# One unit of a state-space scan: the softplus on GpSimd placed behind its multiplications, the C row spread in bf16 parts, the projections paired

## The reference, cut to what matters

```python
xz = x @ in_w.T; xi, z = split(xz)
u = silu(conv(xi) + conv_b)                      # 4 taps along time, 512 channels
dt, Bm, Cm = split(u @ xproj_w.T)                # 16 + 16 + 16 numbers per token
delta = softplus(dt @ dt_w.T + dt_b)
dA = exp(delta * A); dBu = delta * Bm * u        # per channel and per state n = 0..15
h[t] = dA[t] * h[t-1] + dBu[t]; y[t] = sum_n h[t, n] * Cm[t, n]
out = (y + u * Dp) * silu(z) @ out_w.T
```

## Time and profile before

| | |
|---|---|
| time, median of 3 runs | 8230.42 us (8223.12 to 8230.87) |
| the profiled execution | 8213.02 us, its span 8211.7 us |
| busy share of the span | PE 81%, DVE 74%, POOL 48%, ACT 38% |
| granted TensorE clock, mean | 0.89 of full speed |

### The profile page before, as it was taken

The page is one execution under the profiler, slowest core; times in us unless marked ns, Lnnn a source line. Parts: engine busy times, 40 slices in busy tenths (PEclk is TensorE's granted clock), DMA queues, the critical chain, the costliest instruction groups (busy, mean ns, idle before and its releaser), DMA issues. The chain is left out here.

```text
span 8211.7 us, 61601 instructions
## 1 busy us (share of the span) xinstructions
PE 6631.6 (81%) x19212; PEld 3520.3 (43%) x19212; DVE 6111.6 (74%) x7134; ACT 3152.1 (38%) x6327; POOL 3927.4 (48%) x2745
## 2 busy tenths in 40 slices
PE   5888878887788877888778888788887888878887
PEld 3533354333543335433354333543345443444433
DVE  6488965888658885588855888658886588765887
ACT  0255512554125541255412554134531355313553
POOL 3166541665425654255542655426543365433564
PEclk8889898898888988989989999898998988988998
DMA  2000010001100011000110001100001000110001
GB/s 77 19 29 28 27 47 13 29 31 39 32 19 24 31 39 40 13 24 29 39 40 13 29 24 39 40 13 31 24 36 40 16 29 26 36 37 16 29 29 36
DMA packets 211678, 248.50 MB, mean 30 GB/s; under 512 B 140858, under 2 KB 168546, under 8 KB 205412
## 3 DMA queue, kind: packets, MB, share of 16 engines
q1 hardware_dynamic: 211300, 244.04, 9.0%
HBM read 223.98 MB, written 20.03 MB: 30 GB/s over the span
## 5 line engine op out<-in xcount | busy, mean ns | idle before, releaser
L1142 DVE TENSOR_TENSOR_SCAN wk<-ps,wk 128x1024 f32<-128x1024 f32 x1024 | 2333.6, 2280 | 267.9 <-POOL wk L1697 139.6
L1364 PE MATMUL ps<-wk,ident 128*128 128x512 f32 x4096 | 2368.2, 707 | 101.0 <-DVE wk L1163 101.0
L1692 POOL TENSOR_TENSOR wk<-wk 128x1024 f32<-128x1024 f32 x1024 | 2403.2, 2357 | 8.6
L1606 ACT ACTIVATE ps<-wk,Aneg 128x255 f32<-128x255 f32 x4096 | 1700.8, 462 | 1569.2 <-DVE wk L1142 1520.0
L1354 PE MATMUL ps<-wk,ident 48*128 48x256 f32 x2048 | 767.2, 457 | 909.2 <-DVE wk L1151 857.8
L1151 DVE TENSOR_TENSOR wk<-wk,ps 128x1024 f32<-128x1024 f32 x1024 | 1224.9, 1196 | 92.2 <-issue 37.4
L1364 PEld LDWEIGHTS ps<-wk,ident 128*128 128x128 f32 x4096 | 781.2, 211 | 1066.0 <-issue 1063.7
L403 POOL TENSOR_SCALAR rstd<-mv 128x4 f32<-128x4 f32 x146 | 36.1, 247 | 2342.8 <-DVE mv L396 2342.8
L1354 PEld LDWEIGHTS ps<-wk,ident 48*128 48x128 f32 x2048 | 320.6, 196 | 1394.0 <-DVE wk L1151 1243.6
L509 POOL TENSOR_TENSOR wk<-wk 128x4096 f32<-128x4096 f32 x64 | 529.4, 8278 | 294.6 <-ACT wk L631 294.6
L1645 POOL TENSOR_TENSOR wk<-wk 128x1024 f32<-128x1024 f32 x64 | 150.4, 2350 | 1067.1 <-ACT wk L1531 1067.1
(11 more groups left out here) (175 smaller groups left out, 7495.8 us busy)
## 6 DMA issues: line engine op xcount, KB each, us to landing
wk<-bc_scr SPq DMA_DIRECT2D x256, 512.0 KB, 3.6
wk<-in_wgT SPq DMA_DIRECT2D x8, 1536.0 KB, 6.6
wk<-in_wuT SPq DMA_DIRECT2D x8, 1536.0 KB, 9.6
wk<-in_wdn SPq DMA_DIRECT2D x8, 1536.0 KB, 6.5
wk<-in_x SPq DMA_DIRECT2D x18, 512.0 KB, 4.0
o_scr<-wk SPq DMA_DIRECT2D x64, 128.0 KB, 3.0
wk<-o_scr SPq DMA_DIRECT2D x32, 256.0 KB, 3.5
wk<-wf_scr SPq DMA_DIRECT2D x8, 1024.0 KB, 4.8
```

Of the source, the lines that this page charges most:

```text
L1142: V.tensor_tensor_scan(h, in_time(d, flat(decay(m))), h, 0.0, ALU.mult, ALU.add).then_inc(scanned, 1)
L1364: mm = nc.tensor.matmul(bank(j), ident[:], hc[m % RC][:, 2 * j:2 * j + 2, :].rearrange("p e t -> p (e t)"), start=(n == 0), stop=(n == DS ...
L1606: nc.scalar.activation(decay(m)[:, e, rest(d)], dl[g % 2][:, e, rest(d)], ACT.Exp, scale=Aneg[:, d, e, n:n + 1]).then_inc(dA_done, 1)
L1692: nc.gpsimd.tensor_tensor(hb[n], du[g % 2], col(Bb[j % 2][:, n % NB, :]) .broadcast_to([P, NDI, MC]), ALU.mult).then_inc(dbu, 1)
```

## The change

1. GpSimd: `POOL_PRE` is gone. The softplus of the next unit stands behind all 16 multiplications of the unit. The ScalarE and VectorE steps of the softplus move to steps 8 to 11 and to step 10 (`SUM`), behind `conv` of that step. The exponential of the carried factors (ACT, 64 elements) moves from step 0 of its unit to step 13 of the one before.
2. The C row: GpSimd splits rows 32 to 47 of `xd`, which `xpT` now repeats at rows 64 and 96, into three bf16 parts (`part_c`, five small instructions per unit), and `weights` multiplies them by a bf16 selection matrix `sel3` in one bf16 matmul where an f32 one stood.
3. The pieces: the four `LG` are two of 512 columns (steps 2, 3); the two `OUT` become one of 512 columns, made in four halves at steps 4 to 7 and read by one `out_evac` at step 9. `XD` is copied by ScalarE at its step 4, not 3; `LG` by four activations at steps 6 and 7.
4. The woven layer norm moves to steps 10, 12, 14 of unit 6 and 1, 4 of unit 7.
5. Once per launch: `xpT` is cleared by GpSimd and loaded by six DMAs where one was, behind the others.

```diff
-            PRE_PE = {0: (XD, 0), 3: (LG, 0), 4: (LG, 1), 5: (LG, 2), 6: (LG, 3), 8: (X, 0), ...
+            PRE_PE = {0: (XD, 0), 2: (LG, 0), 3: (LG, 1), 8: (X, 0), 9: (X, 1), 10: (X, 2),
-            Z_ACT, XD_ACT, LG_ACT = {0: 0, 1: 1, 2: 2, 3: 3}, 3, {7: 0, 8: 1, 9: 2, 10: 3}
-            OUT_PE, OUT_DVE = {1: 0, 2: 1}, {3: 0, 4: 1}
+            Z_ACT, XD_ACT, LG_ACT = {0: 0, 1: 1, 2: 2, 3: 3}, 4, {6: 0, 7: 1}
+            OUT_PE, OUT_DVE = {4: (0, 0), 5: (0, 1), 6: (1, 0), 7: (1, 1)}, 9
-            SOFT = {10: "abs", 11: "exp", 12: "ln", 13: "less"}
-            SILU, SUM = 15, 13
-            POOL_PRE = {13: ("lost",), 14: ("delta", "du")}
-            CLOSE_DVE = {5: ("stats0",), 7: ("apply0", "stats1"), 9: ("apply1",), 11: ("stats2",), 14: ("apply2",)}
-            CLOSE_POOL = {7: "rstd0", 10: "rstd1", 12: "add", 13: "rstd2"}
+            SOFT = {8: "abs", 9: "exp", 10: "ln", 11: "less"}
+            SILU, SUM, INJ = 15, 10, 13
+            CLOSE_DVE = {10: ("stats0",), 12: ("apply0", "stats1"), 14: ("apply1",), DS + 1: ("stats2",),
+                         DS + 4: ("apply2",)}
+            CLOSE_POOL = {DS + 1: "add", DS + 5: "rstd2"}
...
-                    def out_evac(g, t):
+                    def out_evac(g):
+                        dve.wait_ge(out_mm, g + 1)
+                        y = ytok[:, c * MT:(c + 1) * MT, :]
...
                     def weights(m):
                         if n == 0:
-                            pe.wait_ge(pre_ev, evacuated((XD, g, 0)))
+                            pe.wait_ge(c_part, NPART * (g + 1))
                         if m:
                             pe.wait_ge(cm, m)
-                        nc.tensor.matmul(c_row(), ident[0:XP, row:row + 1].broadcast_to([XP, P]), xd[g % 2][0:XP, :],
+                        nc.tensor.matmul(c_row(), sel3[:, n:n + 1].broadcast_to([XR, P]), xc[g % 2][0:XR, :],
                                          start=True, stop=True).then_inc(c_bc, 1)
...
+                    def part_c(g):
+                        x, parts = xd[g % 2], xc[g % 2]
+                        pool.wait_ge(pre_ev, evacuated((XD, g, 0)))
+                        if g >= 2:
+                            pool.wait_ge(c_bc, DS * (g - 1))
+                        nth = NPART * g
+                        nc.gpsimd.tensor_copy(parts[0:XR, :], x[0:XR, :]).then_inc(c_part, 1)
+                        for q in range(1, PARTS):
+                            rows = slice(XC[q], XR)
+                            pool.wait_ge(c_part, nth + 2 * q - 1)
+                            nc.gpsimd.tensor_tensor(xr[rows, :], (x if q == 1 else xr)[rows, :], parts[rows, :],
+                                                    ALU.subtract).then_inc(c_part, 1)
+                            pool.wait_ge(c_part, nth + 2 * q)
+                            nc.gpsimd.tensor_copy(parts[rows, :], xr[rows, :]).then_inc(c_part, 1)
+                        pool.wait_ge(c_part, nth + NPART)
...
-                            if g + 1 < NU:
-                                for what in POOL_PRE.get(n, ()):
-                                    softplus(g + 1, what)
+                        if g == CLOSE_UNIT:
+                            close_step(1, "rstd0", 0, 0)
+                        if g + 1 < NU:
+                            part_c(g + 1)
+                            for what in ("lost", "delta", "du"):
+                                softplus(g + 1, what)
+                        if g == CLOSE_UNIT:
+                            close_step(1, "rstd1", 0, 0)
```

More of the change, by code:

```diff
@@ L38 @@
 XP = DTR + 2 * DS
+XC = (DTR + DS, 64, 96)
+XR = XC[-1] + DS
 HF, RANK = 1024, 16
@@ L166, in build @@
         inj = [area(at + NDI * MC * RC + i * DS * NDI, DS, NDI) for i in range(2)]
+        at += NDI * MC * RC + 2 * DS * NDI
+        xc = [area(at + i * MC // 2, MC, dt=BF16) for i in range(2)]
+        xr = area(at + MC, MC)
         tt, tl = [area((120 + 4 * i) * KB, NDI, MC) for i in range(2)]
@@ L240, in _ @@
                     sp.dma_start(dst[:], src.broadcast_to([P, src.shape[1]])).then_inc(loaded, 16)
+                sp.wait_ge(blank, 1)
+                for dst, src in SPREAD:
+                    for d in range(2):
+                        sp.dma_start(dst[:, d], src[:, d]).then_inc(loaded, 16)
                 sp.wait_ge(loaded, NLOAD)
@@ L903, in pre_slot @@
                     at = 5 if AT[piece] < NFIRST and AT[piece] % 2 == 0 else 6
-                    return bank(at)[:, 0:XW if piece[0] == X else MC]
+                    return bank(at)[:, 0:{X: XW, LG: 2 * MC, OUT: MT * C}.get(piece[0], MC)]
                 def slot_before(piece):
@@ L1219, in _ @@
                                 finish(g - 1)
-                            if g and n in OUT_DVE:
-                                out_evac(g - 1, OUT_DVE[n])
+                            if g and n == OUT_DVE:
+                                out_evac(g - 1)
                             if g + 2 < NU and n in CONV:
@@ L1235, in _ @@
                         square(s)
-                    for t in range(MT):
-                        out_evac(NU - 1, t)
+                    out_evac(NU - 1)
                     squares = iter(range(UP_FIRST, NF))
-                    dve.wait_ge(out_ev, MT * NU)
+                    dve.wait_ge(out_ev, NU)
                     for name in ("stats0", "apply0", "stats1", "apply1", "stats2", "apply2"):
@@ L1330, in project @@
                             t0 = c * MC + t * P
-                            for k in range(KC):
-                                mm = nc.tensor.matmul(o, xnT[:, k, t0:t0 + P], PxT[:, k, :], start=False,
-                                                      stop=(k == KC - 1))
-                        mm.then_inc(out_mm, 1)
+                            mm = nc.tensor.matmul(o, xnT[:, half, t0:t0 + P], PxT[:, half, :], start=False,
+                                                  stop=(half == 1))
+                        if (t, half) == (MT - 1, 1):
+                            mm.then_inc(out_mm, 1)
                     def ahead_t(piece):
@@ L1462, in _ @@
                             piece = pe_piece(g, n)
-                            if piece:
+                            if g and n in OUT_PE:
+                                project(g - 1, *OUT_PE[n])
+                            elif piece:
                                 pre(piece)
@@ L1467, in _ @@
                         up(s)
-                    for t in range(MT):
-                        project(NU - 1, t)
+                    for part in OUT_PE.values():
+                        project(NU - 1, *part)
                     for s in range(UP_FIRST, NF):
@@ L1672, in _ @@
                     ln_rstd(pool, ecs, 1, 4)
+                    part_c(0)
                     for what in ("lost", "delta", "du"):
```

119 lines of the change are left out of this document (65 added, 54 removed).

## The result

| | before | after |
|---|---|---|
| median of the runs, same chip | 8226.77 us (8213.99 to 8230.87) | 7686.05 us (7684.42 to 7692.83) |
| profiled execution, span | 8213.02, 8211.7 | 7684.65, 7683.3 |
| mean granted clock | 0.89 | 0.90 |

The ratio is 0.9347, 95% interval 0.9331 to 0.9363.

What follows compares the result with a forecast made beforehand. VectorE's own list was taken as the floor, with stalls for GpSimd and TensorE above it. Terms summed to -421, so 7792 us profiled; with 17.4 us up to the median, 7809 us, range 7710 to 7940.

Steps and rivals of the forecast that it cites:

- scans: VectorE's scans at step 15: softplus behind GpSimd's multiplications removes the whole wait in six units of eight sequences, -208 us.
- `out_evac` waits, the last one too: VectorE's projection read, moved to step 9: waits inside units fall from 207.1 to 40 us (-167); last read starts later (+2).
- weighing: VectorE's weighing waits for TensorE: half of 92.2 us goes through the shorter C row and lost half-clock stretch, -46 us.
- `finish`: VectorE's wait for the last state sum: shrinks 4 us in last units and 13 in the others, -17 us.
- fewer, longer reads: VectorE's projection read: one `out_evac` of 512 columns replaces two shorter ones in 56 units, -9 us.
- launch: until the first scan: Start of the launch: five more DMAs with small packets at the end of the awaited list, +3 us (0 to 8).
- collision at L1143, L1147: VectorE's softplus lines at step 10 now come close to GpSimd's "lost" and partly wait for it, +21 us.
- woven layer norm: Layer norm in units 6 and 7: same instructions, colliding with GpSimd as before, 0, within 4 us per sequence.
- TensorE late at step 9: Rival at `out_evac`: TensorE's 26 to 28 us meet VectorE's 26.5 without room; 7860 to 7960 us, chance 0.20.
- Full collision: Rival at VectorE's step 10: the softplus line collides fully with GpSimd's "lost" 56 times; 7919 us, chance 0.08.
- GpSimd still late: Rival on GpSimd's list: something new holds the first multiplication, so the 208 us stay; 8017 us, chance 0.04.
- The clock falls for good: Rival on TensorE: less work drops the clock to half in steps 4 to 7; 8425 us, chance 0.03.

Runs made afterwards that it cites:

- evac8: The changed kernel with `out_evac` at step 8 in place of 9, nothing else; 7929.38 us, ratio 0.9661.
- c_f32: The changed kernel with the C row multiplied in f32 again, ScalarE also waiting for the rows' last reader before copying `XD`; 7735.18 us, ratio 0.9442.
- before_behind: The kernel before with only GpSimd's softplus put behind the multiplications, VectorE's sum staying at step 13; 8012.16 us, ratio 0.978.
- out_early: The changed kernel with the projection's halves back at steps 1 and 2, read at step 4, `LG` at 3 and 4, `XD` copied at 3; 7921.05 us.
- close7: The changed kernel with the woven layer norm whole in unit 7, steps 6 to 10, its copies two steps later, GpSimd's part behind all multiplications; 7708.44 us.
- pool_inline: The changed kernel with GpSimd's softplus back inside its loop at steps 13 and 14, `part_c` with it, except in unit 6; 7778.64 us, ratio 0.9499.
- sum11: The changed kernel with VectorE's softplus sum at step 11, not 10, and the carried factors' exponential at 14; 7635.61 us, ratio 0.9299.
- soft_late: The changed kernel with the softplus later again (ScalarE steps 10 to 13, VectorE's sum at 13), still behind the multiplications; 7849.67 us, ratio 0.9582.
- sum11_close7: The changed kernel with both the softplus sum at step 11 and the woven layer norm whole in unit 7; 7687.56 us, ratio 0.9367.

## Why the prediction was wrong

The sum gave -421 us for the profiled execution and it was -528. A further 16 us of the miss are the step from there to the median: 17.4 us before, 1.4 after. That step was carried over from before without a reason, so these 16 us say nothing on the mechanism.

| term | predicted | measured |
|---|---|---|
| scans | -208 | -208.4 |
| `out_evac` waits, the last one too | -165 | -201.1 |
| weighing | -46 | -72.8 |
| `finish` | -17 | -27.7 |
| fewer, longer reads | -9 | -10.5 |
| wait before the sum, L1143 (no term) | 0 | -11.5 |
| launch: until the first scan | +3 | -3 |
| collision at L1143, L1147 | +21 | +18.4 |
| woven layer norm | 0 | +25.8 |
| convolution's waits (no term) | 0 | -16.7 |

The lines add up to -508; the other 21 are spread over small waits inside and outside the units that no row gives by itself. No single term makes the miss: of the 107 us, 36 are `out_evac`, 27 the weighing, 17 the convolution, 11.5 the wait before the sum and 11 `finish`, against the 26 of the layer norm. `out_evac` is the largest, and the only one of them that was worked out from a list of rows.

**The step that failed** is, first, TensorE's list from `finish` to the last half: "26.1 us for d = 0 ..., with 1 to 2 more for a stretch at half clock", from which 1.2 us of wait per forward read followed. TensorE in order of time in unit 1 after:

```profile
1436.77 3.75 PE L1383 MATMUL ps<-wk,ident 128*128 128x512 f32 x4 [2.71 <-DVE wk L1183]
1440.32 3.17 PE L1329 MATMUL ps<-wk,xpT 128*112 128x256 f32 x8
...
1451.60 0.28 PE L1373 MATMUL ps<-wk,sel 112*128 112x256 bf16 x1 [0.25 <-DVE wk L1171]
1451.72 1.88 PE L1383 MATMUL ps<-wk,ident 128*128 128x512 f32 x4
1453.44 1.03 PE L1347 MATMUL ps<-WcT,wk 128*128 128x256 f32 x4
1454.30 0.59 PE L1351 MATMUL ps<-PxT,xnp 128*128 128x256 f32 x2
1454.91 0.28 PE L1373 MATMUL ps<-wk,sel 112*128 112x256 bf16 x1
...
1464.24 0.59 PE L1351 MATMUL ps<-PxT,xnp 128*128 128x256 f32 x2
```

And VectorE:

```profile
1443.70 1.22 DVE L1171 TENSOR_TENSOR wk<-wk,ps 128x1024 f32<-128x1024 f32 x1 [1.56 <-issue]
...
1463.60 1.19 DVE L1171 TENSOR_TENSOR wk<-wk,ps 128x1024 f32<-128x1024 f32 x1
1464.87 0.69 DVE L1189 TENSOR_TENSOR ytok<-ps,pb 128x512 f32<-128x512 f32 x1
```

Two things are to be seen. First the size: from one start to the next the C row is 0.12 us (0.2 taken), the sum 1.72 to 1.81 (1.85), and the last half ends at 1464.83, 28.2 us behind the end of `finish`. Of these 3.1 are the half clock at the first two pieces (3.55 and 3.01 between starts for 1.8 and 1.7) and 0.25 a wait, so the list at full clock is 24.9 us and not 26.1. Second the form: the delay at the start is not carried to step 9. There is one bank for the C row, so VectorE stops at the weighing of the same stretch (1443.70, 1.56 us), and by step 4 TensorE has caught up: the C row at 1451.60 waits 0.25 us for VectorE. From there C row, sum and half take 0.12 + 1.72 + 0.86 + 0.61 = 3.31 us, to the hundredth VectorE's own step.

A lead is not carried to step 9 either. In unit 2 TensorE starts at full clock, waits 1.02 and twice 0.25 us for VectorE's weighing, and its last half still ends at 1532.20, just ahead of VectorE's read at 1532.24:

```profile
1512.35 0.28 PE L1373 MATMUL ps<-wk,sel 112*128 112x256 bf16 x1 [1.02 <-DVE wk L1171]
...
1531.61 0.59 PE L1351 MATMUL ps<-PxT,xnp 128*128 128x256 f32 x2
```

What counts for `out_evac` is then only the last stretch of TensorE against one step of VectorE. The last half ends 0.04 us ahead of the read in unit 1, so a step earlier the read has to wait a whole step of 3.31, and `evac8` measured 3.39. In a backward unit, without the product with `PxT`, it ends 0.31 us ahead in unit 5 (1735.45 against 1735.76), which gives 3.0, and `evac8` measured 3.0. With the f32 row TensorE's step is 3.45 us, longer than VectorE's, and `c_f32` shows a wait of 1.1 us. So of the predicted 40 us of waits inside units 2.6 are left. That it is so close is luck: with the 3.45 us of `c_f32`, 0.14 more, the forecast of 1.2 us per forward read would have looked right.

**The weighing** was halved by feel. Of the 92.2 us, some 28.6 went with the order alone in `before_behind`; the bf16 row, one of the two reasons of the prediction, gives nothing in `c_f32`. The other 44 are not shown to belong to anything: the new places of the pieces are the natural candidate, but no run moved them alone on top of before, and `out_early`, which puts the projection back, brings back 13.5. Of `finish`, some 16.9 of the 27.7 came with the order.

**The woven layer norm**, put at 0 "since it collides anyway", became 26 us dearer, and `close7` shows by taking all 65 us of it away that it is the collision with GpSimd. It was the largest error against the change. `before_behind`, whose only edit is on GpSimd's list, has L413 16.1 us less busy, so where these instructions fall beside GpSimd counts, and the "0" was a term put at nothing without a reason.

**What held.** The scans' term to 0.4 us, with GpSimd's first multiplication of unit 2 at 1479.21, 17 us ahead of its scan at 1496.07. `part_c` is hidden: its five instructions end at 1454.54, and "lost" waits till 1468.85:

```profile
1454.15 0.39 POOL L1698 CAST wk<-wk 16x256 bf16<-16x256 f32 x1
1468.85 2.36 POOL L1669 TENSOR_TENSOR wk<-wk 128x1024 f32<-128x1024 f32 x1 [14.31 <-ACT wk L1554]
```

The collision of L1143 with "lost" cost 18 us for 21, which is partly luck: the new meetings cost 29 us (2.1 in unit 0, where 1.1 was taken, and 0.3 to 0.4 in units 1 to 5), and 11 came back from unit 6, where L1123 took 2.63 us in the trace of before and L1143 takes 1.21. The Trainium skill (SBUF — State Buffer, "Who interferes with whom") has the two engines exclude each other for a whole instruction. The runs agree: VectorE's instruction ends a fixed time behind the GpSimd instruction that it met, 1.08 us in `pool_inline` (1486.47 against 1485.39) and 1.09 in unit 0 of before (1422.93 against 1421.84 in the earlier trace rows). So it waits for all of what is left of the other, and the cost hangs on when the two meet: 0.4 us (L1143's 1.67 for some 1.22) as a mean in the changed kernel, next to none in `sum11`. The full price of the rule, 131 us, did not come because "lost" was nearly over at 40 of the 48 meetings, which is the argument that the prediction had against this rival.

**The rivals.** TensorE late at step 9: wrong, by the 2.6 us. Full collision: wrong here; in `pool_inline` it is real. GpSimd still late: wrong; it is what `soft_late` makes, at the start of a unit. The clock falls for good: wrong. Windows of unit 1 after, from `finish` and from the next C row on, up to `out_evac`:

```profile
1436.60:1443.30 6.70, 6.53 (x12) 3.60 (x13) 5.54 (x4) 1.67 (x4) 6.54 (x5) 0.53 0.00 0
```

```profile
1443.40:1464.80 21.40, 21.02 (x68) 10.75 (x66) 21.09 (x13) 17.06 (x35) 10.54 (x13) 1.00 0.15 51
```

One short stretch at half clock stands behind TensorE's wait of 2.71 us for `finish`, and then the clock is 1.00 with the bf16 C row as it was in the earlier trace rows with the f32 one. By the Trainium skill (TensorE: Matmul & The Clock Gate, "HAM oscillation — how this bites in real kernels") a fall in each round was to be feared; the trace agrees in six of the seven units of the second sequence that have this wait, with a mean clock of 0.53 (unit 1) and 0.75 to 0.78 (units 3 to 7) in the 6.7 us behind `finish`, and 1.00 in unit 2 alone. The price is small: 1.56 us at the weighing of unit 1, at most 0.22 in the others, and nothing at `out_evac`.

## What to carry to other kernels

Where two engines hand one buffer back and forth, a delay is not simply carried forward along a list: ask where the handover stops it, and compare the steady steps of both, here 3.31 and 3.31 us; neither a delay nor a lead passes it, so a sum from the last sync point over seven steps mis-sizes the end. When waits are gone, what is left is the overlap of elementwise instructions of VectorE and GpSimd, and it changes with every shift by a step, because VectorE's instruction waits for whatever is left of GpSimd's: moving the softplus sum by one step brought 52 us, and two moves of the layer norm that looked as harmless cost 20 and 25. A move that removes a collision has to be weighed with the copy or `rstd` that it makes late on a third engine.

## What was not expected of the hardware

An instruction on GpSimd also grows when it meets one of VectorE's: L1734 took 3.32 us for 2.35 beside L1143 and L1147. It ended 2.20 us behind the L1143 that had started before it (1485.39 against 1483.19), so it too waited the other out. A `TENSOR_SCALAR` of 256 elements with one SBUF input, L432, took 5.45 us for four beside GpSimd where 2.21 had stood. In `close7` a stage far from the edit took on a stretch at the 1.2 GHz level, ahead of the first convolutions of seven of the eight sequences; the periods agree to 0.1 us from the second on (952.3), as the changed kernel's do (948.9). The same stage has it in six of the eight sequences of `c_f32`, in five of `sum11_close7` and in one of `sum11`, where that period is 947.6 for 942.1. So a stretch like this can come back with each turn of the loop or only in some turns, and it moves the total by 3 to 6 us each time. Why this stage and not another is open.
